# Second layers of 20 more hidden pairs in three fp32r products, their split weights in the staged W1's home, and the first turn in another order

## The reference, cut to what matters

```
x = x + xattn(ctx, layernorm(x))     # in_proj, causal conv of 4 taps, silu, x_proj, softplus(dt),
                                     # scan over 256 steps with 16 states, * silu(layernorm(x))
h = layernorm(x)
shared = mean over 2 experts of  relu(h @ w1 + b1) @ w2 + b2
gates  = softmax(h @ router_w + router_b), best 6 of 32 kept and renormalized
routed = sum over 32 experts of  gates[e] * (relu(h @ w1[e] + b1[e]) @ w2[e] + b2[e])
x = x + shared + routed
```

## Time and profile before

| what | value |
|---|---|
| median of 3 runs | 391.04 us (388.28 to 392.22) |
| the profiled execution, time | 388.61 us |
| its span, first to last instruction | 386.8 us |
| PE busy | 353.3 us (91% of the span) |
| DVE, ACT, POOL busy | 262.5, 223.3, 197.6 us |
| mean granted TensorE clock | 0.978 |

### The profile page before, as it was taken

One profiled execution on the slowest core, in us unless ns is written; L12 is line 12 of the kernel. 1 busy time (PEld: TensorE's weight loads), 2 busy tenths in 40 slices (PEclk: granted clock), 3 DMA queues, 4 the chain that ended last, 5 costly groups with the idle time before them and its releaser, 6 DMA issues.

```text
span 386.8 us, 6569 instructions
## 1 busy us (share of the span) xinstructions
PE 353.3 (91%) x2306; PEld 322.6 (83%) x2306; DVE 262.5 (68%) x448; ACT 223.3 (58%) x560; POOL 197.6 (51%) x159
## 2 busy tenths in 40 slices
PE   6439889992899979999999999999999998999997
PEld 4228768892799959899999899999999898999996
DVE  3588798687788746769988466799864616545444
ACT  2689965556565254728744456487523445667672
POOL 0389886067886300259993102599841024454542
PEclk9959999998799999999999999999999999999999
DMA  7496950423942314399723215985222234232320
GB/s 229 160 329 180 337 160 2 147 76 94 348 152 68 84 48 109 102 305 269 191 72 91 74 56 153 298 257 169 81 83 82 69 107 143 81 107 86 97 69 27
DMA packets 30686, 54.07 MB, mean 140 GB/s; under 512 B 3290, under 2 KB 8638, under 8 KB 30654
## 3 DMA queue, kind: packets, MB, share of 16 engines
q1 hardware_dynamic: 30654, 53.67, 46.0%
HBM read 52.34 MB, written 1.31 MB: 139 GB/s over the span
## 4 chain that ended last, share of the span: by engine, by line
PE 63%; DVE 13%; ACT 8%; issue 7%; POOL 4%; DMA 2%; DVEq 0%; SPq 0%; POOLq 0%; ACTq 0%
PE acc L640 26%; PE z L673 9%; PE z L675 9%; PE z L674 9%; PE dA L640 4%; DVE dA L930 4%; POOL bu L1104 3%; ACT dA L753 2%; POOL ya L1120 1%; PE z L546 1%; DVE hg L1044 1%; ACT w1h L694 1%; DVE cv L887 1%; DMA bt<-bc 1%; PE dA L565 1%
## 5 line engine op out<-in xcount | busy, mean ns | idle before, releaser
L640 PE MATMUL acc<-hg,w 128*128 128x256 f32 x564 | 135.1, 382 | 8.9 <-DVE hg L1044 8.2
L640 PEld LDWEIGHTS acc<-hg,w 128*128 128x128 f32 x564 | 103.2, 191 | 21.2 <-DVE hg L1044 8.3
L673 PE MATMUL z<-xh,w1l 128*128 128x256 f32 x376 | 117.8, 313 | 0.3 <-DVE xl L1005 0.3
L1104 POOL TENSOR_TENSOR bu<-bt,du 128x512 f32<-128x512 f32 x64 | 81.1, 1280 | 59.5 <-DVE du L924 43.7
L843 ACT ACTIVATE z<-z,par 128x256 f32<-128x256 f32 x176 | 70.5, 438 | 68.5 <-PE z L675 66.9
L1044 DVE TENSOR_TENSOR hg<-z,gt 128x512 f32<-128x512 f32 x88 | 60.4, 687 | 71.8 <-ACT z L843 68.5
L675 PE MATMUL z<-xh,w1h 128*128 128x256 f32 x376 | 105.7, 281 | 0.0
L674 PE MATMUL z<-xl,w1h 128*128 128x256 f32 x376 | 105.6, 281 | 0.0
L930 DVE TENSOR_TENSOR_SCAN dA<-dA,bu 128x512 f32<-128x512 f32 x60 | 73.3, 1222 | 12.5 <-POOL bu L1104 6.7
L673 PEld LDWEIGHTS z<-xh,w1l 128*128 128x128 f32 x376 | 70.9, 189 | 3.4 <-issue 1.5
L674 PEld LDWEIGHTS z<-xl,w1h 128*128 128x128 f32 x376 | 71.2, 189 | 1.5
(11 more groups left out here) (165 smaller groups left out, 440.0 us busy)
## 6 DMA issues: line engine op xcount, KB each, us to landing
...
```

Of the source, the lines that this page charges most:

```text
L640: mm = pe.matmul(total(b, k), weights, h, start=t + n == 0 and (k == 0 or final_batch(b)), stop=last, skip_group_check=True)
L673: pe.matmul(z[p % ZB][:, i, :], w1l[:, t, one], high[:, k, :], start=k == 0, stop=False)
L1104: pool.tensor_tensor(bu[:, r, :].rearrange("p (j l) -> p j l", j=2), bt[:, c % BRING], du[:, k:k + 1, :].broadcast_to([P, 2, L]), ALU.mult ...
```

## The change

It makes `SPLIT` a table by batch: in batch 1 the pairs 16 to 23, in batch 2 the pairs 4, 7, 10, 13 and 16 to 23, in batch 3 all as before; that is 20 pairs more, none of them pair 1. `nth_split` counts over all batches. w2l and w2h now lie where stage lay; bt and ct have a home of their own. In batch 0's turn the doubled scan units move by one pair (from pairs 6, 10, 13 to 7, 11, 14), "xall" of batch 2 and "dtl" and "dt" go one pair later, "var" of batch 1 goes behind the second layer, "logits" of batch 1 goes from behind pair 22 to ahead in pair 23, and "top" goes to pair 23. "turn" and "gates_out" of batch 0 go to pair 4, the first use of its gates' low part to pair 5, and SP writes and reads back those gates at its pair 7 rather than before its pair 0; two loads of rows come two pairs later.

```diff
@@ -56,9 +56,9 @@
 RING = 6
 EARLY = 3
 B2_AT = 4
-B2_AT0 = 6
+B2_AT0 = 5
 GLOW_AT = 2
-GLOW_AT0 = 6
+GLOW_AT0 = 5
 SINGLE0 = NP - NPR
 
 
@@ -78,10 +78,10 @@
         ("dtl", 21), ("dt", 21), ("sp", 22), ("over", 22), ("delta", 23)]
 TURN = [(n, at, 1) for n, at in UNITS + ZGATE + BACK] + [(n, at, 2) for n, at in NEXT]
 BEHIND = ("var", "logits", "xall", "dt", "turn", "spread")
-AHEAD = [("xall", 1), ("var", 1)]
-
-
-UNIT_AT = [3, 4, 5, 6, 6, 7, 8, 9, 10, 10, 11, 12, 13, 13, 14, 15]
+AHEAD = [("xall", 1), ("turn", 0), ("logits", 1)]
+
+
+UNIT_AT = [3, 4, 5, 6, 7, 7, 8, 9, 10, 11, 11, 12, 13, 14, 14, 15]
 TURN0 = [(("bu", 0, 0), 2, 1), (("bu", 0, 1), 2, 1)]
 for _c in range(NC):
     for _k in range(KD):
@@ -92,9 +92,9 @@
 TURN0 += [("stats", 4, 1), ("rs1", 5, 1), ("nb1", 6, 1), ("zz", 7, 1), ("ez1", 8, 1), ("ez2", 9, 1), ("ez3", 10, 1), ("zmul", 12, 1),
           ("xin", 15, 2), ("cv0", 15, 2), ("yfold", 15, 1), (("taps", 1, 2), 16, 2), ("x1", 16, 1), ("x1s", 16, 1),
           (("taps", 2, 3), 17, 2), (("taps", 3, KC), 17, 2), ("econv", 17, 2), ("uclip", 18, 2), ("usig", 18, 2), ("u", 19, 2),
-          ("mean", 20, 1), ("centre", 20, 1), ("sq", 20, 1), ("sqs", 20, 1), ("xall", 20, 2), ("var", 21, 1), ("dtl", 21, 2), ("dt", 21, 2),
-          ("r2", 21, 1), ("norm", 21, 1), ("xh", 22, 1), ("logits", 22, 1), ("xl", 22, 1), ("sp", 22, 2), ("over", 22, 2), ("top", 22, 1),
-          ("ex", 23, 1), ("gates", 23, 1), ("delta", 23, 2), ("turn", NP, 1), ("gates_out", NP, 1)]
+          ("mean", 20, 1), ("centre", 20, 1), ("sq", 20, 1), ("sqs", 20, 1), ("var", 21, 1), ("xall", 21, 2), ("dtl", 22, 2), ("dt", 22, 2),
+          ("r2", 21, 1), ("norm", 21, 1), ("xh", 22, 1), ("xl", 22, 1), ("logits", 23, 1), ("top", 23, 1), ("ex", 23, 1), ("gates", 23, 1),
+          ("sp", 23, 2), ("over", 23, 2), ("delta", 23, 2), ("turn", NP, 1), ("gates_out", NP, 1)]
 
 
 HEAD = [(("warm", None, 11), 0), ("xin", 0), (("warm", None, 16), 0), ("cv0", 0), (("taps", 1, KC), 0), (("warm", "conv_done", 6), 0), ("econv", 0), ("uclip", 0),
@@ -123,12 +123,10 @@
         [("dtl", 1)],
         [("gt0", 0), ("sp", 1), ("over", 1), ("delta", 1)],
         [("xall", 1), ("dt", 1), ("spread", 0)],
-        [],
-        [("turn", 0)],
-        [("gates_out", 0)]]
-
-
-SPLIT = []
+        [("turn", 0), ("gates_out", 0)]]
+
+
+SPLIT = {1: range(16, NP), 2: [4, 7, 10, 13, *range(16, NP)], B - 1: range(NP)}
 BIG = 2.0 ** 63
 
 
@@ -152,12 +150,13 @@
         w1h = sb("w1h", [P, NT, KD * P], F32R)
         w1l = sb("w1l", [P, NT, KD * P], F32R)
         w2 = sb("w2", [P, RING, 2, DX])
-        with nc.sbuf_tensor("bt", [P, BRING, 2, L], F32) as bt, nc.sbuf_tensor("ct", [P, BRING, 2, L], F32) as ct:
+        bt = sb("bt", [P, BRING, 2, L])
+        ct = sb("ct", [P, BRING, 2, L])
+        with nc.sbuf_tensor("stage", [P, WRING, WCH * KD * P], F32) as stage:
             pass
         w2l = sb("w2l", [P, 4, 2, DX], F32R)
         w2h = sb("w2h", [P, 4, 2, DX], F32R)
         gt = sb("gt", [P, NG, L])
-        stage = sb("stage", [P, WRING, WCH * KD * P])
 
         def pv(name):
             return par[:, PAR[name][0]:PAR[name][1]]
@@ -338,11 +337,11 @@
 
         def split(b, p):
 
-            return p in SPLIT or (type(b) is int and b == B - 1)
+            return p in SPLIT.get(b, ())
 
         def nth_split(b, p):
 
-            return b * len(SPLIT) + sum(split(b, q) for q in range(p + 1))
+            return sum(split(f, q) for f in range(b + 1) for q in range(NP) if (f, q) <= (b, p))
 
         def final_batch(b):
             return type(b) is int and b == B - 1
@@ -431,6 +430,11 @@
                 for g in (2 * half, 2 * half + 1):
                     eng.dma_start(gt[:, g, :], gates_d[b % 2, g * GEXP:(g + 1) * GEXP, :].rearrange(
                         "(e o) l -> e o l", o=1).broadcast_to([GEXP, GROW, L])).then_inc(ld_g[half], 16)
+
+            def spill_gates(b):
+                eng.wait_ge(S["gates_done"], b + 1)
+                eng.dma_start(gates_d[b % 2], gT[0:NR, :]).then_inc(S["spilled"], 16)
+                eng.wait_ge(S["spilled"], 16 * b + 16)
 
             for i in range(3):
                 load_w1(i)
@@ -458,19 +462,21 @@
             for c in range(BRING):
                 load_bc(1, c)
             for b in range(B):
-                eng.wait_ge(S["gates_done"], b + 1)
-                eng.dma_start(gates_d[b % 2], gT[0:NR, :]).then_inc(S["spilled"], 16)
-                eng.wait_ge(S["spilled"], 16 * b + 16)
                 if b:
+                    spill_gates(b)
                     wait_hg(eng, b - 1, SINGLE0 + NPART - 1)
                     load_gates(b, 0)
                     wait_hg(eng, b - 1, NP - 1)
-                load_gates(b, 1)
+                    load_gates(b, 1)
                 for p in range(NP):
+                    if b == 0 and p == 7:
+                        spill_gates(b)
+                        load_gates(b, 1)
                     if 0 < b < B - 1 and p < BRING - 1:
                         load_bc(b + 1, p + 1)
-                    if b < B - 1 and p in (4, 6, 8, 10):
-                        load_bc(b + 1, BRING + (p - 4) // 2)
+                    at = p - (4 if b else 6)
+                    if b < B - 1 and at in (0, 2, 4, 6):
+                        load_bc(b + 1, BRING + at // 2)
                     if b + 2 < B and p == NP - 2:
                         spill_bc(b + 2)
                     if b + 2 < B and p == NP - 1:
```

## The result

Over 20 runs of each in turns, the changed kernel takes 393.37 us (389.83 to 396.0) and the kernel before 388.99 us (388.01 to 392.42). The ratio is 1.0094, 95% interval 1.0072 to 1.0117: slower by 0.9%, 3.7 us by the ratio. The prediction was 385.9 us, and the time lies above its range. (The median of 391.04 us that it started from was of three runs and lies 2.05 us above that of these 20; from 388.99 its sum would have given 383.9. The kernel before has two groups of runs: of 35 later ones, 21 with a mean clock of 0.973 or more had a span of 387.1 us on average, 14 at 0.964 or 0.965 one of 390.1.)

A forecast was written before the change was run, and what follows sets the result against it. It took PE to set the time beside batches 1 and 2. Gains of 0.7 + 0.7 + 1.4 + 2.3 = 5.1 us took 388.6 to 383.5; with 2.4 for the runs' median, 385.9 us, range 380.5 to 390.5.

The forecast's parts named there:

- The gain of a split pair on PE, 0.345 us: Each of 20 pairs spares PE 0.345 us: 2.76 in each tail, 1.38 in batch 2's units, 6.9 in all.
- I count the whole 1.4 us: In batch 2's units DVE and POOL have free time for the four splits, so the whole 1.4 us is kept.
- No wait of PE in batch 2's units: Sign to look for in the new profile: PE waits for nobody during batch 2's scan units.
- The rule on the shared port: DVE and GpSimd lock shared ports, so some new hl take 1.3 us; if it shows in batch 1's tail, 386.6 us.
- Rare: The median hl time, 0.681 us against a longest of 1.30, says that lengthening by the shared port is rare.
- Batch 1's tail, 0.7 kept: In batch 1's tail PE waits about 2 us for `final`, so 0.7 us of the 2.76 spared is kept.
- Batch 2's tail, 2.3 kept: In batch 2's tail ACT has room; 0.4 us is taken off for "xs", so 2.3 of 2.76 us is kept.
- The first turn, 0.7: In batch 0's turn the 8.17 us wait goes but nearly all returns as other waits of PE; 0.7 us is gained.
- The rival of the clock: PE's clock falls in the new 4.2 us wait before "var"; the first turn loses 0.7 us: 387.3 us, chance 0.18.
- ACT carries batch 1's tail: ACT's added 8.6 us all lie on the way to the next turn's first decay: 395.2 us, chance 0.06.
- The chances: Whole kernel: faster by over 1% 0.64, within 1% 0.31, slower 0.05.

The follow-up runs named there:

- skip_both: Changed kernel with POOL's w2l and DVE's hl left out for batch 2's pairs 4, 7, 10 and 13; ratio 0.9962 to the kernel before.
- skip_hl: Changed kernel with DVE's hl left out for batch 2's pairs 4, 7, 10 and 13, w2l still formed; ratio 0.9998 to the kernel before.
- turn_only: Changed kernel with only the last batch split, so the kernel before with the new first turn; ratio 0.9971 to the kernel before.
- mid_only: Changed kernel with splits only in batch 2's pairs 4, 7, 10, 13 and the last batch; ratio 0.9996 to the kernel before.
- all_three: no_mid with the second unit's scan, product and fold at pair 2, the third unit's decay a pair later, "xin" behind the second layer; ratio 0.9976.
- no_mid: Changed kernel without the splits of batch 2's pairs 4, 7, 10 and 13; ratio 0.9995 to the kernel before.
- xin_behind: Changed kernel with splits in batch 2's pairs 16 to 23 and the last batch alone, "xin" behind pair 12's second layer; ratio 0.9962.
- xin_hot: xin_behind with 16 idle products of ones by ones on PE ahead of the first turn's variance; ratio 0.9964 to the kernel before.
- all_tail2: all_three without batch 1's splits; ratio 0.9960 to the kernel before.

## Why the prediction was wrong

- *The gain of a split pair on PE, 0.345 us.* Right in batch 2's units: skip_both shows 1.37 us for four pairs. It was taken between neighbouring pairs with nothing between their layers, and in the tails it is less. The tails of skip_hl, where the clock is 1.00:

```profile
217.58:246.87 29.29, 26.98 (x211) 24.82 (x209) 24.09 (x48) 21.47 (x54) 12.56 (x9) 1.00 0.37 107
297.82:325.01 27.19, 24.36 (x203) 23.70 (x201) 19.49 (x42) 17.30 (x40) 12.36 (x10) 1.00 0.32 94
```

  PE is busy 1.6 us less than before in batch 1's tail (28.58) and 2.3 less in batch 2's (26.68), not 2.76 each. Between the starts of second layers in turn_only and skip_hl, waits taken off, the pairs of batch 1's tail with no step of the table between spare 0.31 to 0.37 us, the three with such steps -0.02 to 0.12.
- *Batch 2's units, "I count the whole 1.4 us".* This is the step that failed most: +2.6 instead of -1.4. It compared free time over the whole window (10.5 us on DVE, 12.8 on POOL) with the work added. But the free time lies at its end. The windows of DVE alone, from the kernel before:

```profile
244.11:275.54 31.43, 27.93 (x39) 1.00 0.73 225
275.54:294.35 18.81, 11.82 (x16) 1.00 0.30 82
```

  Of the 10.5 us free, 7.0 come after 275.5; of the 3.5 before it, 1.9 lie ahead of the first scan at 246.0, and from there DVE has no pause over 0.2 us for 29.5 us, while it makes up for its late start. The changed trace has it without a pause from 246.85 to 288. Each hl pushed the rest back by 1.35 us on average, and the end of the block with it. x1 then met two w2l (2.92 instead of 0.88 us), PE waited 2.81 us, and the clock fell after it (0.94 over that tail). mid_only separates the two: the late block by itself left PE no wait there; with x1's 2.0 us more, and the first hl of the tail ahead of it in DVE's list (0.69 us), it did. "No wait of PE in batch 2's units" was wrong too: the 0.8 us for w2l of pair 4 and these 2.81.
- *The rule on the shared port.* Its price for one hl, 0.66 us, was about right where it was paid (0.22 to 0.87 us, in nine of the 20 new hl). In sum the 20 new hl took 5.4 us more than 0.68 each, not 13. But x1's two instructions, which the rule was not applied to, took 3.0 us more in the two batches (4.8 instead of 1.8), and it was those of batch 2 that PE waited for. The free time that was to carry it lay elsewhere, as above. The Trainium skill, page "SBUF — State Buffer", section "SBUF: two separate sides", names DVE instructions with two SBUF inputs against GpSimd ones that read SBUF, and the runs agree: hl and x1 are lengthened, scan, "prod" and hg, which read PSUM, are not (1.22, 0.69, 0.68 us beside a busy POOL). "Rare" was wrong for the new places: the earlier trace rows came from the last batch, where POOL has no scan unit to do.
- *Batch 1's tail, 0.7 kept.* The waits named are there, 0.24 for "dt" (I had 0.8) and 1.49 for `final` (I had 2), but a place was left out, the gates before "turn" (0.2 to 0.6), and PE spares 1.6 and not 2.76 us. With the clock at 1.00 the tail is 0.7 longer (29.3), not shorter: 1.6 us less work and 2.3 us of waits. Where the clock falls it is 1.9 longer. The list that holds `final` was rightly seen as ACT's with DVE's; all_three shows which steps of it.
- *Batch 2's tail, 2.3 kept.* 0.8 to 0.9 was kept in the profiles with all eight splits there in which "x1s" held PE by 1.2 us or less (27.2 to 27.3 against 28.06): 2.3 us less work, 1.4 us more of waits. In no_mid PE waits 0.93 us for "xs" instead of 0.29, 0.56 before "turn" and 1.4 for `final` instead of 1.1. I had looked at one of these places.
- *The first turn, 0.7.* Right in size in the profile (81.0 to 80.3 us), and the wait changed its place, as it said: PE waits 2.13 us for "sqs" (I had 4.2) and, unforeseen, 3.75 for "xin". The size is partly luck, since a fall of the clock there decides 1.5 to 3 us. One place was missed, "xin" behind "zmul", and the clock's fall went with it: 7 us at 0.50 from 114 on, where before it was 94 to 100. The rival of the clock named "sqs", where it fell in four profiles of other versions and not in this one.
- *The rival "ACT carries batch 1's tail"* was not what happened. ACT's load rose there by 6.7 of the 8.6 us reckoned (21.47 against 14.79), and overlapped.
- *The chances.* By the shares that the text names, faster by over 1% is 0.03 + 0.20 + 0.29 + 0.06 = 0.58, not 0.64, and within 1% is 0.36, not 0.31.

A version faster than both: splits in batch 2's tail alone with the new first turn, 389.76 us against 391.06 beside it, ratio 0.9959 (0.9927 to 0.9991). Three more with the same splits, xin_behind, xin_hot and all_tail2, stand at 0.9960 to 0.9964. The new first turn without any new split (0.9971) is not told from them.
